# First batch's transposed rows made inside stage one in memory of their own, last residual ahead of them, odd x rows in the context's memory

## What is computed

```python
# block 1: each token has one of 4 experts by its id; all three weights of expert e are ctx[e] (512 x 512)
h = layernorm(x)
g = silu(h @ ctx[e].T); u = h @ ctx[e].T
x = x + tanh(g_xattn) * ((g * u) @ ctx[e].T)      # e = expert of the token's id
# block 2: each batch picks 2 of 6 experts by the mean of its normalised rows
h = layernorm(x)
p = softmax(h.mean(over the batch's tokens) @ gate_W.T); take the top 2, weights scaled to sum 1
for each chosen expert s: eo_s = gelu(h @ W1[s] + b1[s]) @ W2[s] + b2[s]      # 512 -> 352 -> 512
x = x + tanh(g_ffn) * sum_s weight_s * eo_s
```

## Time and profile before

| | |
|---|---|
| median of 3 runs | 301.01 us (300.83 to 301.47) |
| profiled execution | 301.36 us, of which the profile's span is 299.8 us |
| instructions | 4432 |
| PE busy | 280.9 us (94%) |
| DVE busy | 207.2 us (69%) |
| ACT busy | 110.6 us (37%) |
| POOL busy | 67.5 us (23%) |
| chain that ended last | PE 85%, DVE 6%, DMA 3%, ACT 3%, issue 1%, POOL 1% |

### The profile page before, as it was taken

One profiled execution on the slowest core, in us unless ns is written; L12 is line 12 of the kernel. 1 busy time (PEld: TensorE's weight loads), 2 busy tenths in 40 slices (PEclk: granted clock), 3 DMA queues, 4 the chain that ended last, 5 costly groups with the idle time before them and its releaser, 6 DMA issues.

```text
span 299.8 us, 4432 instructions
## 1 busy us (share of the span) xinstructions
PE 280.9 (94%) x1390; PEld 224.7 (75%) x1390; DVE 207.2 (69%) x457; ACT 110.6 (37%) x195; POOL 67.5 (23%) x93
## 2 busy tenths in 40 slices
PE   1978999999999999999979699999999999999995
PEld 0756888888888888878767477878788787887874
DVE  7897677877887897788677655577475864746133
ACT  1682232222232225534365174163542353432010
POOL 3541045545444555332232000000000000000000
PEclk9999999999999999999999999999999999999998
DMA  6931022231254222139402209540294305730003
GB/s 216 374 116 35 0 72 70 70 106 72 79 160 150 72 95 82 64 76 309 151 35 76 102 7 318 205 140 0 58 327 168 116 2 156 229 143 0 0 0 140
DMA packets 21489, 34.44 MB, mean 115 GB/s; under 512 B 1864, under 2 KB 10062, under 8 KB 21468
## 3 DMA queue, kind: packets, MB, share of 16 engines
q1 hardware_dynamic: 18400, 24.16, 25.1%
q0 software_dynamic: 3040, 9.98, 10.3%
q10 hardware_dynamic: 28, 0.02, 0.0%
HBM read 24.97 MB, written 9.19 MB: 114 GB/s over the span
## 4 chain that ended last, share of the span: by engine, by line
PE 85%; DVE 6%; DMA 3%; ACT 3%; issue 1%; POOL 1%; SPq 1%; POOLq 0%
PE bank L918 36%; PE bank L894 13%; PE bank L896 13%; PE bank L895 13%; PE bank L909 3%; PE bank L902 2%; PE bank L1000 2%; ACT ctx_hi L759 2%; DMA raw_ctx<-x_scratch 1%; DMA x_scratch<-x_ring,put_rows 1%; DVE raw_ctx L667 1%; DVE ctx_lo L621 1%; DVE w_raw L489 1%; POOL x_ring L377 1%; PE bank L957 1%
## 5 line engine op out<-in xcount | busy, mean ns | idle before, releaser
L894 PE MATMUL bank<-ctx_lo,w_hi 128*128 128x512 f32 (+1 forms) x96 | 38.5, 401 | 1.6 <-DVE ctx_lo L621 1.6
L894 PE MATMUL bank<-w_lo,ctx_hi 128*128 128x512 f32 (+1 forms) x96 | 38.1, 397 | 0.0
L896 PE MATMUL bank<-ctx_hi,w_lo 128*128 128x512 f32 (+1 forms) x96 | 37.7, 393 | 0.0
L895 PE MATMUL bank<-ctx_hi,w_hi 128*128 128x512 f32 (+1 forms) x96 | 37.7, 392 | 0.0
L895 PE MATMUL bank<-w_hi,ctx_hi 128*128 128x512 f32 (+1 forms) x96 | 37.4, 390 | 0.0
L896 PE MATMUL bank<-w_hi,ctx_lo 128*128 128x512 f32 (+1 forms) x96 | 37.4, 390 | 0.0
L659 DVE TENSOR_SCALAR ctx_hi<-raw_ctx,mix 128x512 fp32r<-128x512 f32 x16 | 7.9, 495 | 30.8 <-ACT raw_ctx L811 30.8
L647 DVE TENSOR_TENSOR w_lo<-w_raw,w_hi 128x512 fp32r<-128x512 f32 (+2 forms) x24 | 27.8, 1174 | 1.0 <-ACT w_hi L803 1.0
L811 ACT ACTIVATE raw_ctx<-bank,b1T 128x512 f32<-128x512 f32 x16 | 11.0, 689 | 46.2 <-PE bank L896 44.5
L744 ACT ACTIVATE a<-bank 128x512 f32<-128x512 f32 x19 | 11.4, 599 | 43.1 <-PE bank L918 43.1
L739 ACT ACTIVATE aT_hi<-bank 128x512 fp32r<-128x512 f32 x18 | 10.8, 598 | 41.4 <-PE bank L909 41.4
(11 more groups left out here) (158 smaller groups left out, 533.6 us busy)
## 6 DMA issues: line engine op xcount, KB each, us to landing
raw_ctx<-x_scratch SPq DMA_DIRECT2D x16, 257.0 KB, 3.7
raw_ctx<-in_ctx SPq DMA_DIRECT2D x4, 1024.0 KB, 9.5
w_raw<-in_L_ffn_W SPq DMA_DIRECT2D x8, 512.0 KB
out<-raw_ctx SPq DMA_DIRECT2D x16, 256.0 KB, 2.1
w_raw<-in_L_ffn_W SPq DMA_DIRECT2D x8, 448.0 KB, 5.7
w_raw<-in_L_ffn_W SPq DMA_DIRECT2D x8, 256.0 KB, 4.0
w_raw<-in_L_ffn_W SPq DMA_DIRECT2D x8, 192.0 KB
x_ring<-in_x,get_rows POOLq DMA_INDIRECT x19, 3.5
```

The costliest lines, as they stand in the source:

```text
L894: pe.matmul(dst, s_hi, m_lo, start=first, stop=False)
L895: pe.matmul(dst, s_hi, m_hi, start=False, stop=False)
L896: return pe.matmul(dst, s_lo, m_hi, start=False, stop=last)
```

## The change

- The transposed normalised rows of batch 0 (`h2T_hi0`, `h2T_lo0`) get memory of their own, over and just behind the raw context's. So ACT's pass over the banks in step 14 writes the high parts as well as the sums (`ffn_h_high(0)` in the place of `token_sums`), and the four high copies after the last product go.
- DVE makes the four low parts at the ends of steps 15, 16, 17 and 18, one each; in step 15 behind `choose(0)`, in step 17 ahead of the split of the weights.
- After the last product DVE has `residual(18)` directly behind `residual(17)`. W2's low part follows the first `weigh` of batch 0.
- The x rows of batches 1 and 3 lie behind `a2_hi` in the memory of the context's high parts; those of batches 0 and 2 and all else of stage two stay in the raw context's memory.
- For batch 0 alone, PE makes the two pairs of transpositions of batch 1 six matmuls later each, `logits(1)` after the first block of `hidden(0, 1)` and the spreading after its second.

```diff
-        ctx_hi = sb("ctx_hi", [P, E * KD * F1], FP32R)
-        ctx_lo = sb("ctx_lo", [P, E * KD * F1], FP32R)
-        raw_ctx = sb("raw_ctx", [P, E, KF1, D])
-        arena = raw_ctx[:, :, :, :].rearrange("p e k d -> p (e k d)")
         X1B = TT * DS
-        x1b = arena[:, 0:2 * X1B]
-        h2 = arena[:, 2 * X1B:2 * X1B + TT * D]
...
-        h2T_hi = ctx_hi[:, 0:2 * KD * S]
-        h2T_lo = ctx_lo[:, 0:2 * KD * S]
+        CTX = E * KD * F1 * 4
+        FIRST = [X1B * 4, TT * D * 4, 2 * S * 4, KD * S * 4, KD * S * 4]
...
+        place = [2 * CTX + sum(FIRST[:i]) for i in range(len(FIRST))]
+        x1_even = at("x1_even", [P, X1B], FP32, place[0])
+        h2 = at("h2", [P, TT * D], FP32, place[1])
+        act = at("act", [P, 2, S], FP32, place[2])
+        h2T_hi0 = at("h2T_hi0", [P, KD * S], FP32R, place[3])
+        h2T_lo0 = at("h2T_lo0", [P, KD * S], FP32R, place[4])
+        x1_odd = at("x1_odd", [P, X1B], FP32, (2 * KD + FC) * S * 4)
+
+        def x1_of(b, start, size):
+            return (x1_odd if b % 2 else x1_even)[:, start:start + size]
+
+        def h2T_of(b, k):
+            place = slice((b % 2) * (KD * S) + k * S, (b % 2) * (KD * S) + (k + 1) * S)
+            if b == 0:
+                place = slice(k * S, (k + 1) * S)
+                return h2T_hi0[:, place], h2T_lo0[:, place]
+            return ctx_hi[:, place], ctx_lo[:, place]
...
 DVE
-            def ffn_h_low(b, banks):
-                for k in range(KD):
+            def ffn_h_low(b, banks, ks=range(KD)):
+                for k in ks:
...
                 if j == PREP + 3:
                     choose(0)
+                if PREP + 3 <= j:
+                    ffn_h_low(0, o_ps, [j - PREP - 3])
                 if j == PREP + 5:
                     split_low(0, 0, 0)
                     split_low(0, 0, 1)
             a_low(TILES - 1, hT_ps, hT_hi, hT_lo)
             residual(TILES - 2)
-            ffn_h_low(0, o_ps)
             residual(TILES - 1, aT_ps)
             dve.wait_ge(pads_made, 4)
-            split_low(0, 0, 2)
 
             def batch(b, more):
                 for c in range(FC):
                     weigh(b, 0, c)
+                    if b == 0 and c == 0:
+                        split_low(0, 0, 2)
                     if c < 2:
                         split_low(b, 1, c)
...
 ACT
-            def token_sums():
-                for k in range(KD):
-                    sc.wait_ge(h2T_done, k + 1)
-                    sc.activation(x1b[:, X1B + k * S:X1B + (k + 1) * S], o_ps[k][:, :], ACT.Identity,
-                                  accum_out=hsum[:, k:k + 1]).then_inc(sums_done, 1)
...
                 if j == PREP + 2:
-                    token_sums()
+                    ffn_h_high(0, o_ps)
...
             split_high(0, 0, 2)
-            sc.wait_ge(y_done, TILES)
-            ffn_h_high(0, o_ps)
             sc.wait_ge(gwT_copied, 1 + FC)
...
 PE
-            def hidden(b, s, between=None):
+            def hidden(b, s, more=False):
...
-                    if between and c == 0:
-                        between(b + 1)
+                    if more and b == 0 and c == 0:
+                        logits(b + 1)
+                    if more and c == (1 if b == 0 else 0):
+                        spread_mix(b + 1)
...
             def batch(b, more):
                 hidden(b, 0)
                 output(b, 0, full)
-                if more:
+                if more and b > 0:
                     transpose_h2(b + 1, (0, 1))
                 output(b, 0, [FC - 1], range(0, TT // 2))
                 if more:
+                    transpose_h2(b + 1, (2, 3) if b > 0 else (0, 1))
+                output(b, 0, [FC - 1], range(TT // 2, TT)).then_inc(pair_done, 1)
+                if more and b > 0:
+                    logits(b + 1)
+                elif more:
                     transpose_h2(b + 1, (2, 3))
-                output(b, 0, [FC - 1], range(TT // 2, TT)).then_inc(pair_done, 1)
-                if more:
-                    logits(b + 1)
-                hidden(b, 1, spread_mix if more else None)
+                hidden(b, 1, more)
```

More of the change, by code:

```diff
@@ L115, in flamingo_kernel, with at @@
         t_ps, hid_ps, o_ps = banks[0:2], banks[2:4], banks[4:8]
-        ctx_hi = sb("ctx_hi", [P, E * KD * F1], FP32R)
-        ctx_lo = sb("ctx_lo", [P, E * KD * F1], FP32R)
-        raw_ctx = sb("raw_ctx", [P, E, KF1, D])
-        arena = raw_ctx[:, :, :, :].rearrange("p e k d -> p (e k d)")
         X1B = TT * DS
-        x1b = arena[:, 0:2 * X1B]
-        h2 = arena[:, 2 * X1B:2 * X1B + TT * D]
-        act = arena[:, 2 * X1B + TT * D:2 * X1B + TT * D + 2 * S].rearrange("p (c t) -> p c t", t=S)
-        h2T_hi = ctx_hi[:, 0:2 * KD * S]
-        h2T_lo = ctx_lo[:, 0:2 * KD * S]
+        CTX = E * KD * F1 * 4
+        FIRST = [X1B * 4, TT * D * 4, 2 * S * 4, KD * S * 4, KD * S * 4]
+        region = (nc.sbuf_base + 31) // 32 * 32
+        sb("region", [P, (2 * CTX + sum(FIRST)) // 4])
+        def at(name, shape, dt, offset):
+            return nc.alloc_sbuf_tensor_at(name, shape, dt, offset=region + offset)
+        ctx_hi = at("ctx_hi", [P, E * KD * F1], FP32R, 0)
+        ctx_lo = at("ctx_lo", [P, E * KD * F1], FP32R, CTX)
+        raw_ctx = at("raw_ctx", [P, E, KF1, D], FP32, 2 * CTX)
+        place = [2 * CTX + sum(FIRST[:i]) for i in range(len(FIRST))]
[13 more added lines that the diff above has]
+            return ctx_hi[:, place], ctx_lo[:, place]
         w_raw = [sb(f"w_raw{s}", [P, WN]) for s in range(2)]
@@ L258, in flamingo_kernel @@
         pads_made, waited = sem("pads_made"), sem("waited")
-        tiles_landed, warmed, sums_done = sem("tiles_landed"), sem("warmed"), sem("sums_done")
+        tiles_landed, warmed = sem("tiles_landed"), sem("warmed")
         ctx_rest_done, ctx_lo_by_act = sem("ctx_rest_done"), sem("ctx_lo_by_act")
@@ L296, in load_x1 @@
                 for t in range(TT):
-                    sp.dma_start(x1b[:, bass.ds((b % 2) * X1B + t * DS, DS)],
+                    sp.dma_start(x1_of(b, t * DS, DS),
                                  x1_rows[bass.ds(b * S + t * P, P), :]).then_inc(x1_here[t], 16)
@@ L321, in store @@
                     sp.dma_start(out.rearrange("b s d -> (b s) d")[bass.ds(b * S + t * P, P), :],
-                                 x1b[:, bass.ds((b % 2) * X1B + t * DS, D)]).then_inc(out_stored, 16)
+                                 x1_of(b, t * DS, D)).then_inc(out_stored, 16)
             sp.wait_ge(ctxT_done, E * KD)
@@ L612, in ffn_normalise @@
                     dve.wait_ge(x1_here[t], 16 * b + 16)
-                    at = (b % 2) * X1B + t * DS
-                    dve.tensor_scalar(h2[:, t * D:(t + 1) * D], x1b[:, bass.ds(at, D)], x1b[:, bass.ds(at + D, 1)],
-                                      x1b[:, bass.ds(at + D + 1, 1)], ALU.subtract, ALU.mult).then_inc(h2_ready, 1)
-            def ffn_h_low(b, banks):
-                for k in range(KD):
+                    dve.tensor_scalar(h2[:, t * D:(t + 1) * D], x1_of(b, t * DS, D), x1_of(b, t * DS + D, 1),
+                                      x1_of(b, t * DS + D + 1, 1), ALU.subtract, ALU.mult).then_inc(h2_ready, 1)
+            def ffn_h_low(b, banks, ks=range(KD)):
+                for k in ks:
                     dve.wait_ge(h2T_hi_done, KD * b + k + 1)
-                    place = bass.ds((b % 2) * (KD * S) + k * S, S)
-                    dve.tensor_tensor(h2T_lo[:, place], banks[k % len(banks)][:, :], h2T_hi[:, place].bitcast(FP32),
+                    hi, lo = h2T_of(b, k)
+                    dve.tensor_tensor(lo, banks[k % len(banks)][:, :], hi.bitcast(FP32),
                                       ALU.subtract).then_inc(h2T_lo_done, 1)
@@ L665, in finish @@
                     dve.wait_ge(o_done, TT * b + t + 1)
-                    place = x1b[:, bass.ds((b % 2) * X1B + t * DS, D)]
+                    place = x1_of(b, t * DS, D)
                     dve.tensor_tensor(place, o_ps[t][:, :], place, ALU.add).then_inc(o_taken, 1)
@@ L780, in ffn_h_high @@
                     sc.wait_ge(h2T_done, KD * b + k + 1)
-                    sc.activation(h2T_hi[:, bass.ds((b % 2) * (KD * S) + k * S, S)], banks[k % len(banks)][:, :],
+                    sc.activation(h2T_of(b, k)[0], banks[k % len(banks)][:, :],
                                   ACT.Identity, accum_out=hsum[:, k:k + 1]).then_inc(h2T_hi_done, 1)
-            def token_sums():
-                for k in range(KD):
-                    sc.wait_ge(h2T_done, k + 1)
-                    sc.activation(x1b[:, X1B + k * S:X1B + (k + 1) * S], o_ps[k][:, :], ACT.Identity,
-                                  accum_out=hsum[:, k:k + 1]).then_inc(sums_done, 1)
             def exponents(b):
@@ L1014, in logits @@
                 if isinstance(b, int) and b == 0:
-                    pe.wait_ge(sums_done, KD)
+                    pe.wait_ge(h2T_hi_done, KD)
                     pe.wait_ge(hT_lo_done, PREP + 4)
@@ L1037, in hidden @@
```

(9 more changed lines are left out.)

## The result

| | before | changed |
|---|---|---|
| median of 20 runs | 301.46 us (300.3 to 304.3) | 300.16 us (299.59 to 301.59) |
| profiled execution: time / span | 301.36 / 299.8 us | 300.6 / 299.0 us |
| PE busy | 280.9 us (94%) | 283.6 us (95%) |

The ratio of the times is 0.9942, 95% interval 0.9920 to 0.9964: 1.7 us faster (the medians are 1.3 us apart). The forecast was 3.1 us and 297.9 us, in a range from 297.0 to 299.3. The sign was right, the time lies outside the range.

A forecast was written before the change was run, and what follows sets the result against it. PE was taken as the bound, full from 190 us, with 4.5 us idle in two gaps where the stages meet. 1.76 - 0.95 - 0.3 + 2.77 - 0.1 = 3.2, rounded to 3.1; 301.01 - 3.1 = 297.9 us, range 297.0 to 299.3.

The forecast's parts named there:

- Other places in memory: New addresses of the tensors that the change moves: claimed to cost nothing that a row shows, no term given.
- Gap A: PE's idle time between stage one's last product and `hidden(0, 0)`: goes whole, 1.76 us gained.
- The halves: DVE's four low halves, one each in steps 15 to 18: cost PE 0.95 us, bounds 0.3 and 2.5.
- The first delay: Step 15's low half ahead of `normalise(17)`: transposition and second product both move, PE loses 0.5 to 0.6 us.
- the wait for the mix: Step 16's half delays DVE's copy of the mix from 134.04 to 134.98; PE 0.95 us late in all.
- Wait at `output(0, 0)`: PE waits for the second weighed block, behind W2's low part on DVE: 0.3 us lost, bounds 0 and 0.9.
- Gap B: PE's idle time ahead of batch 1's transposition, waiting for normalised rows: goes whole, 2.77 us, rows early by 1.75.
- POOL's 1.45 us: POOL's power of the last tile's deviation, 2.02 us beside W2's low part, gets 1.45 us shorter.
- Logits and mix later: PE's later logits and mix around `hidden(0, 1)`, with the gelu table's return: 0.1 us lost, bounds 0 and 0.6.
- The rule on the table's drain: Skill's drain of about 1.38 us per table switch, 2.66 in all; by it the gain would be 1.7 us.
- Weights of batch 1: W2's last piece split at 185.6, low half done by 189, needed 8.4 us after 188.4: no wait.
- rivals: Halves nearly free 0.12; DVE bounds four steps 0.10; table switch 0.05; row chain unmoved 0.04; every half paid twice 0.04.

The follow-up runs named there:

- e8_after_pad480: The changed kernel with 480 bytes more behind its common region; measured 298.20 us, ratio 0.9875.
- e3_before_pad32: The kernel before with 32 bytes of unused padding ahead of the weights' memory, nothing else; measured 302.86 us, ratio 1.0046.
- e7: The changed kernel with 96 bytes more behind its region, but PE's order for batch 0 as in the kernel before; measured 299.47 us.

## Why the prediction was wrong

The terms of the sum were right; the step that failed is one sentence ahead of it: "Other places in memory cost nothing that a row shows; I leave it at that." The rows of before could not show it, as they held one layout only, and a cost unseen should have been a term with bounds. It was worth 2.1 us: from the first transposition to the last matmul the changed kernel takes 273.49 us, and with all tensors behind the region back at their old places within 512 bytes (e8_after_pad480) 271.37. Against before's 274.92 the change without the shift gains 3.55 us.

Point by point, in those executions:
- **Gap A**, 1.76 us: gone, as forecast.
- **The halves**, forecast 0.95: PE's transposition behind the mix starts at 136.02 instead of 134.26. Less the 1.04 us by which it was late already and the 0.03 that the place in memory costs on this way (e3_before_pad32) that is 0.69; e8_after_pad480 gives 0.70. Mechanism and steps (15 and 16 cost, 17 and 18 don't) were right. The first delay was 0.28 instead of 0.5 to 0.6 us (the transposition at 130.01 in the earlier trace rows comes 14.70 us behind the start of those of batch 0's rows, in e8_after_pad480 14.98), and the wait for the mix makes the rest.
- **Wait at `output(0, 0)`**, forecast 0.3: 0.35.
- **Gap B**, 2.77: gone, with 3.2 us of room (168.47 less 165.3) where 1.75 was reckoned. POOL's 1.45 us was as forecast; the order of PE's pieces was not needed for it (e7).
- **Logits and mix later**, forecast 0.1: no wait. The rule on the table's drain did not show in these rows of the changed kernel:

```profile
175.74 1.28 ACT L770 ACT_TABLE_LOAD   x1
...
177.36 1.30 ACT L824 ACTIVATE act<-bank,b1T 128x512 f32<-128x512 f32 x2
```

  The gelu starts 1.62 us after the load's start; the Trainium skill's 2.66 us ("ScalarE: Activation LUTs", "What ACT_TABLE_LOAD costs") would not fit in between.
- **Weights of batch 1**: ACT waited 2.98 us for W2's last piece (186.76, forecast 185.6), against 0.79 in the earlier trace rows, as PE came earlier and the load did not. Nobody on PE waited for it.
- **The sum** of what was measured is 1.76 - 0.69 - 0.35 + 2.77 = 3.5 us. Put to its old places the kernel ran in 298.2 us, near the 297.9 forecast; as it is, 2.1 of the 3.5 are given back, 1 to 6 ns at each matmul of stage two and 0.027 us at each tile of stage one.
- **"From 190 us on PE should be as full as before"** held, and was the wrong thing to look at.

None of the rivals is what happened. Two further things shift the comparison. The first 20 us differ from execution to execution, the first transposition starting anywhere from 20.76 to 21.84 us. It seems to hang on the moment at which TensorE's clock comes up: the same four transpositions start at 10.93 us in both profiles and take 0.77 us before and 1.09 in the changed kernel. That put 0.70 us on this pair of profiles. And six of before's 20 runs took 302.8 to 304.3 us, as executions with a fall of the clock do; without them its median is 301.10 instead of 301.46, near the 301.01 that I started from, and the gain 0.9 us. So the falls work for the change, and the 1.7 us are partly theirs. What stays open is which distances between two operands are good ones and why, and if the change delays the start on average: the ten profiles of kernels that hold the change have a mean of 21.5 us, the four of kernels without it 21.05, too few to say.

## What to carry to other kernels

- When a change moves tensors, compare the distance from start to start of the same matmuls in a stretch without waits, before looking for waits. A few bytes of padding are a cheap test and, where the stream is full, a cheap gain: here 96 bytes ahead of the ring were worth 1.2 us of 300, and 480 behind the region 2.1.
- To place added work on an engine, look for the idle time behind its latest deadline, not for its average load: the same instructions cost 0.7 us ahead of work that PE waited for and nothing that shows right behind it.
- A hole of nearly 3 us in PE's stream cost more than its length in some executions here, since the clock was lower behind it; of two holes in a row, closing the second alone made the first as long (2.7 us), with the same fall of the clock.

## What the runs showed of the hardware that was not expected

- The distance of 128x512 fp32 matmuls in a full stream depends on where their operands lie within 512 bytes: 0.2274 to 0.2331 us for the same instructions, and 6.400 to 6.493 us for a tile of 24 matmuls and 8 transpositions. Moving one operand by 32 bytes took the distance in `hidden(0, 0)` from 0.2312 to 0.2325 or 0.2328 us, moving both by 32 left it at 0.2312.
- TensorE's granted clock was 0.50 for some 3 to 7 us after idle times of 2.7 and 2.8 us in some executions, and stayed at 1.00 after one of 2.6 us in another.
